# Destination lanes in source order: where a graph kernel scatters, gathers and counts

## The reference

```python
gate = silu(edge_attr @ F1W + F1b) @ F2W + F2b
gate = gate + (emb[atom_z[src]] * (emb[atom_z[dst]] @ adapt)).sum(-1, keepdims=True)
msg  = gate * h[dst] * (cw * node_mult[dst])[:, None]
agg  = segment_sum(msg, src); tot = segment_sum(node_mult[dst], src)
# then four attention layers over the same edges, an MLP layer with segment_sum over dst,
# and two more: out = segment_sum(x[row] * norm[:, None], col), norm from deg = count of edges per row
```

## Time and profile before

| | us |
|---|---|
| median of 3 runs | 19813.48 |
| lowest and highest | 19801.2, 19824.42 |
| span of the profiled execution, first to last instruction | 17009.2 |
| time of the profiled execution around its span | not listed in the profile |
| median less span | 2804.3 |

### The profile page before, as it was taken

The page is one execution under the profiler, slowest core; times in us unless marked ns, Lnnn a source line. Parts: engine busy times, 40 slices in busy tenths (PEclk is TensorE's granted clock), DMA queues, the critical chain, the costliest instruction groups (busy, mean ns, idle before and its releaser), DMA issues. The chain is left out here.

```text
span 17009.2 us, 405783 instructions
## 1 busy us (share of the span) xinstructions
PE 9949.2 (58%) x119882; PEld 7747.5 (46%) x119882; DVE 11124.4 (65%) x27289; ACT 5234.6 (31%) x15775; POOL 9202.6 (54%) x10645
## 2 busy tenths in 40 slices
PE   2000047777777647974896599569926666433454
PEld 1000024444444237864785488458824444333324
DVE  6830046777776767985897599759954555466757
ACT  0000012222222014651564266236613333221120
POOL 7777777777777104431442244124427777585270
PEclk9755555555555569987997899699958777756656
DMA  3833357677678437645663666276612222134445
GB/s 117 327 93 102 102 87 80 85 85 85 85 86 79 80 102 209 176 126 150 186 176 91 196 176 176 56 227 176 175 48 61 65 65 65 45 129 143 148 152 161
DMA packets 2548685, 2116.02 MB, mean 124 GB/s; under 512 B 418374, under 2 KB 2314590, under 8 KB 2541593
## 3 DMA queue, kind: packets, MB, share of 16 engines
q1 hardware_dynamic: 2225086, 1439.58, 31.2%
q0 software_dynamic: 309216, 539.46, 19.4%
q10 hardware_dynamic: 14216, 135.01, 2.3%
HBM read 1290.57 MB, written 726.03 MB: 119 GB/s over the span
## 5 line engine op out<-in xcount | busy, mean ns | idle before, releaser
L627 POOL DMA_INDIRECT attend_rows<-key_rows,attend_fetch_now x1824 | 1747.7, 958 | 2056.5 <-PE attend_seg L1670 1729.3
L1714 ACT ACTIVATE attend_hot<-attend_lane_hot,attend_share 128x128 f32<-128x128 fp8e4 x7296 | 2228.5, 388 | 1209.9 <-DVE attend_share L1737 976.5
L627 POOL DMA_INDIRECT edges_rows<-raw,edges_perm_now x1824 | 2007.5, 1101 | 629.1 <-issue 602.4
L627 POOL DMA_INDIRECT keys_rows<-table,keys_staged x1564 | 1658.6, 1060 | 471.0 <-issue 471.0
L1670 PE MATMUL attend_seg<-attend_rows,attend_hot 128*128 128x49 f32 x14592 | 1816.8, 278 | 122.9 <-ACT parts_layer L1718 85.7
L1670 PEld LDWEIGHTS attend_seg<-attend_rows,attend_hot 128*128 128x128 f32 x14592 | 1734.3, 195 | 207.1 <-issue 201.9
L627 POOL DMA_INDIRECT mlp_xin<-table,mlp_staged x1564 | 1511.3, 966 | 472.7 <-issue 469.3
L1044 PE MATMUL edges_ps_t<-ident,edges_attr 128*40 128x128 f32 x1824 | 425.4, 413 | 1861.6 <-ACT edges_attr L1099 1833.9
L633 POOL DMA_INDIRECT messages<-spread_out,spread_place_now x912 | 1027.9, 1127 | 385.9 <-issue 276.5
L1657 PE MATMUL attend_qx<-attend_table,attend_oht 128*128 128x90 bf16 x21888 | 1087.8, 207 | 124.8 <-DMA attend_oht<-src_hots 113.0
L1481 POOL COPY expand_table<-k 128x156 bf16 x912 | 289.3, 317 | 1602.4 <-issue 947.3
(11 more groups left out here) (517 smaller groups left out, 23761.4 us busy)
## 6 DMA issues: line engine op xcount, KB each, us to landing
key_rows<-expand_out SPq DMA_DIRECT2D x304, 624.0 KB
attend_ea<-edge_attrs SPq DMA_DIRECT2D x912, 160.0 KB
tally_rows<-messages SPq DMA_DIRECT2D x152, 864.0 KB, 4.8
attend_table<-q SPq DMA_DIRECT2D x1832, 67.5 KB
expand_oht<-dst_hots SPq DMA_DIRECT2D x304, 384.0 KB, 4.8
attend_oht<-src_hots SPq DMA_DIRECT2D x912, 128.0 KB
attend_lane_hot<-src_hots_by_edge SPq DMA_DIRECT2D x912, 128.0 KB
raw<-keys_rows ACTq DMA_DIRECT2D x46, 2176.0 KB
```

Source lines behind the costliest of these rows:

```text
L627: return nc.gpsimd.indirect_dma_start(out=out, out_offset=None, in_=table, in_offset=bass.IndirectOffsetOnAxis(ap=index, axis=0))
L1714: ins = nc.scalar.activation(hot[p][:, u, c, :], lane_hot8[r][:, u, c, :], ACT.Copy, scale=share[p][:, u, c:c + 1])
```

## The change

The edge pass no longer scatters destination lanes or counts. It keeps the lanes in source order in a tile `k.dl_a`, stored once at its end as a table of granules (`k.dloc_a`). The one-hot stage gathers that table by a new index, `k.origin`, the inverse of `k.place`: four gathers for a chunk of four supertiles, then a store to `k.dloc_b`, then the load as before; the store and load are issued by ScalarE. The index is made in the key stage, behind the sort, like the place map but with the roles of the two orders exchanged. The counts are made there too, behind the index, in 92 half chunks of 17 columns from lanes and blocks in order of the input. The clearing of `k.dloc_b` goes.

```diff
 def edge_keys
-        nowhere = sb("nowhere", [P, NS], BF16)
+        HC = C // 2
+        lane_hot = [both[:, b, 0:HC * P // 2].bitcast(BF16).rearrange("p (c l) -> p c l", l=P) for b in range(2)]
+        block_hot = [both[:, b, HC * P // 2:HC * (P + NT) // 2 + 1].bitcast(BF16)[:, 0:HC * NT].rearrange("p (c t) -> p c t", t=NT) for b in range(2)]
...
-            for q in range(GR):
-                sp.dma_start(k.dloc_b.rearrange("(p q n) a -> p q (n a)", p=P, q=GR)[:, q], nowhere[:]).then_inc(s_out, 16)
...
+            with pe.Fori(0, CHUNKS) as n:
+                for b in range(2):
+                    pe.wait_ge(s_lanes[b], n + 1)
+                    for c in range(HC):
+                        ins = t.matmul(hist[b][:, 0:NT], lane_hot[b][:, c, :], block_hot[b][:, c, :], start=(c == 0), stop=(c == HC - 1))
+                    ins.then_inc(s_cnt, 1)
...
+            dve.sem_inc(s_inv, 1)
...
+            for q in range(4):
+                dve.wait_ge(s_mm, 13 + q)
+                ch.step(v.tensor_scalar(level[0:UT, :], small[0:UT, 256:256 + KB], uoff[0:UT, q:q + 1], None, ALU.subtract))
+                ch.done(v.tensor_copy(jump[0:UT, :], small[0:UT, 320:320 + KB]))
+                for half in (slice(0, P // 2), slice(P // 2, P)):
+                    ch.done(v.tensor_tensor(under, rows_of(level[0:UT, :], P // 2), bc(k.iota[0:UT, half], KB), ALU.is_le))
+                    ch.done(v.tensor_tensor(under, under, rows_of(jump[0:UT, :], P // 2), ALU.mult))
+                    ch.done(v.tensor_reduce(at[0:UT, q, half], under, AX, ALU.add))
...
+            ch.done(v.tensor_tensor(k.origin[:], k.origin[:], part, ALU.add))
+            ch.done(v.memset(k.count[0][:], 0.0))
+            with dve.Fori(0, CHUNKS) as t:
+                for b in range(2):
+                    here = bass.ds((t * 2 + b) * HC, HC)
+                    v.tensor_tensor(lane_hot[b], bc(loc[1][:, here], P), rows_of(k.iota[:], HC), ALU.is_equal)
+                    v.tensor_tensor(block_hot[b], bc(blk[1][:, here], NT), rows_of(k.iota[:, 0:NT], HC), ALU.is_equal).then_inc(s_lanes[b], 1)
+                for b in range(2):
+                    dve.wait_ge(s_cnt, t * 2 + b + 1)
+                    ch.done(v.tensor_tensor(k.count[0][:], k.count[0][:], hist[b][:, 0:NT], ALU.add))
 def edge_pass
-                if live(n, 2):
-                    o = (s - 2) % TURN
-                    pool.wait_ge(s_dl, n - 1)
-                    pool.wait_ge(s_place, n - 1)
-                    for u in range(CHR):
-                        scatter(nc, k.dloc_b, place_now[:, o, u:u + 1], dl[o][:, u, :], NS * P - 1).then_inc(s_scat[o], 16)
...
+            sp.wait_ge(s_dl, CHN)
+            sp.dma_start(k.dloc_a.rearrange("(p r) c -> p (r c)", p=P), k.dl_a[:]).then_inc(s_kept_dl, 16)
+            sp.wait_ge(s_kept_dl, 16)
...
-                    pe.wait_ge(s_hot, n + 1)
-                    after(pe, s_added, n)
-                    for c in range(COL):
-                        ins = mm(ps_n[:, 0:NT], hot_d[:, c, :], hot_j[:, c, :], start=(c == 0), stop=(c == COL - 1))
-                    ins.then_inc(s_cnt, 1)
...
-                    after(act, s_scat[b], t * (16 * CHR))
-                    a(dl[b][:].rearrange("p u c -> p (u c)"), rows[b][:, :, DL], ACT.Copy).then_inc(s_dl, 1)
+                    a(k.dl_a[:, bass.ds(n * COL, COL)], rows[b][:, :, DL], ACT.Copy).then_inc(s_dl, 1)
...
-                    v.tensor_copy(place_now[:, s], k.place[:, bass.ds(n * CHR, CHR)]).then_inc(s_place, 1)
...
-                        dve.wait_ge(s_cnt, n)
-                        ch.done(v.tensor_tensor(k.count[0][:], k.count[0][:], ps_n[:, 0:NT], ALU.add))
-                    ch.step(v.tensor_tensor(hot_d[:], bc(r[:, :, DL], P), rows_of(k.iota[:], COL), ALU.is_equal))
-                    ch.done(v.tensor_tensor(hot_j[:], bc(r[:, :, DB], NT), rows_of(k.iota[:, 0:NT], COL), ALU.is_equal))
 def dst_hots
+            for n in range(2 * HALF):
+                after(pool, s_taken, n - 1)
+                for u in range(n * HCH, (n + 1) * HCH):
+                    gather(nc, lanes[:, u, :], k.dloc_a, k.origin[:, u:u + 1]).then_inc(s_got[n % 2], 16)
...
+            def put(n, b, t):
+                at = bass.ds(n * HCH, HCH)
+                act.wait_ge(s_got[b], (t + 1) * (16 * HCH))
+                act.sem_inc(s_taken, 1)
+                act.dma_start(k.dloc_b.rearrange("(u p) c -> p u c", p=P)[:, at, :], lanes[:, at, :]).then_inc(s_put[b], 16)
+            def load(n, b, t):
+                act.wait_ge(s_put[b], (t + 1) * 16)
+                act.wait_ge(s_bro, n * HCH - b * HCH + 1)
+                act.dma_start(row[b][:], k.dloc_b.rearrange("(a u p) c -> a u (p c)", a=1, p=P)[:, bass.ds(n * HCH, HCH), :]).then_inc(s_row[b], 16)
+            put(0, 0, 0)
+            with act.Fori(0, HALF - 1) as t:
+                put(t * 2 + 1, 1, t)
+                load(t * 2, 0, t)
+                put(t * 2 + 2, 0, t + 1)
+                load(t * 2 + 1, 1, t)
...
-                    sp.dma_start(lanes[:, at, :], k.dloc_b.rearrange("(u p) c -> p u c", p=P)[:, at, :]).then_inc(s_lanes, 16)
```

More of the change, by code:

```diff
@@ L423, in _ @@
             ins.then_inc(s_perm, 1)
+            pe.wait_ge(s_inv, 1)
+            t.transpose(small[0:NT, 128:128 + NT], base[0][0:NT, 0:NT], k.ident[0:NT, 0:NT]).then_inc(s_mm, 1)
+            for q in range(4):
+                pe.wait_ge(s_inv, 2 + q)
+                t.matmul(small[0:UT, 256:256 + KB], ended[0:NT, q * UT:(q + 1) * UT], base[1][0:NT, :], start=True, stop=True)
+                t.matmul(small[0:UT, 320:320 + KB], ended[0:NT, q * UT:(q + 1) * UT], steps[0:NT, :], start=True, stop=True).then_inc(s_mm, 1)
+            pe.wait_ge(s_inv, 6)
+            for q in range(4):
+                ins = t.transpose(wide[:, q * UT:(q + 1) * UT], at[0:UT, q, :], k.ident[0:UT, 0:UT])
+            ins.then_inc(s_mm, 1)
+            with pe.Fori(0, CHUNKS) as n:
[4 more added lines that the diff above has]
+                    ins.then_inc(s_cnt, 1)
         @block.vector
@@ L582, in _ @@
             ch.done(v.tensor_scalar(listed, listed, float(E), None, ALU.min))
+            dve.sem_inc(s_inv, 1)
+            dve.wait_ge(s_mm, 12)
+            ch.done(v.tensor_tensor(shift[0:NT, 0:NT], small[0:NT, 128:128 + NT], base[1][0:NT, 0:NT], ALU.subtract))
+            ch.step(v.tensor_scalar(begun[0:NT, :], uiota[0:NT, :], first[1][0:NT, :], None, ALU.is_ge))
+            ch.step(v.tensor_copy(steps[0:NT, 0:1], shift[0:NT, 0:1]))
+            ch.step(v.tensor_tensor(steps[0:NT, 1:NT], shift[0:NT, 1:NT], shift[0:NT, 0:NT - 1], ALU.subtract))
@@ new lines, in _ @@
+            ch.done(v.tensor_tensor(tot[1][0:NT, :], final_b[0:NT, :], lane[0:NT, :], ALU.add))
+            ch.done(v.tensor_scalar(ended[0:NT, :], uiota[0:NT, :], tot[1][0:NT, :], None, ALU.is_gt))
+            ch.done(v.tensor_tensor(ended[0:NT, :], begun[0:NT, :], ended[0:NT, :], ALU.subtract))
+            dve.sem_inc(s_inv, 1)
+            for q in range(4):
+                dve.wait_ge(s_mm, 13 + q)
[5 more added lines that the diff above has]
+                    ch.done(v.tensor_reduce(at[0:UT, q, half], under, AX, ALU.add))
+                ch.done(v.tensor_tensor(at[0:UT, q, :], at[0:UT, q, :], gran[0:UT, q, :], ALU.add))
+                dve.sem_inc(s_inv, 1)
@@ L1214, in _ @@
                 step(CHN + s, s, LOOPS)
-            dve.wait_ge(s_cnt, CHN)
-            ch.done(v.tensor_tensor(k.count[0][:], k.count[0][:], ps_n[:, 0:NT], ALU.add))
             dve.wait_ge(s_ev, CHN)
```

70 lines of the change are left out of this document (33 added, 37 removed).

## The result

| | median us | lowest, highest | runs |
|---|---|---|---|
| before | 19807.34 | 19799.03, 19824.42 | 4 |
| after | 19640.99 | 19627.19, 19660.36 | 4 |

The account below looks back on a forecast made before the run. GpSimd was taken to bound the key stage and edge pass, VectorE's comparisons the one-hot stage. Edge pass -260, final store +3, one-hot stage +221 and key stage +200 make +164 us on 19813.5: 19978 us, range 19790 to 20150.

Parts of the forecast that it names:

- the gain of the edge pass: Edge pass: 210 us for late records plus 60 less 10 gives 260 us, bounds 120 and 443.
- a floor of 12.78 us a step: Edge pass: the loop of TensorE and ScalarE allows no less than 228 x 12.78 = 2914 us.
- Which I carry unchanged: Whole kernel: the median's 2804.3 us above the profiled span was taken to stay the same.
- Key stage: Key stage: new VectorE instructions with two SBUF inputs hold GpSimd's gathers, about +200 us, bounds 0 and 260.
- Rival D: Key stage: the new comparisons don't hold the gathers, so it costs nothing; 19777 us in all, chance 0.07.
- the scatters': Edge pass: without scatters GpSimd stops being the bound; 210 us of late records credited in full.
- The count: Edge pass: removing it lets VectorE catch up faster after stalls, 60 us, bounds 0 and 119.
- Rival C: Edge pass: stalls are absorbed and it runs at its 12.78 us loop, winning 443 us; 19795 us in all, chance 0.12.
- Rival B: Edge pass: DMA queues take over, broadcast-load stalls leave a gain of only 120 us; 20118 us in all, chance 0.15.
- One-hot stage: One-hot stage: 456 gathers at 1.25 us on GpSimd set its length, 588 us for 367, +221 us.
- rival E: One-hot stage: three DMAs in sequence per chunk make 1.5 us a gather, +330 us; 20087 us in all, chance 0.11.
- Nothing else in the span is edited: Whole kernel: only the key stage, edge pass and one-hot stage are touched by the change.

Follow-up runs that it names:

- e1: The kernel before, unedited, profiled a second time, on a slow chip: 19367.05 us.
- e12: The kernel before, unedited, once more on a third slow chip: 19915.18 us.
- e18: Changed kernel with the count back in the edge pass (lanes only), and a step's eight gathers parted by a wait, quick chip: 0.9875 of before.
- e10: The whole change, unedited, against the kernel before, on a slow chip: 1.0088.
- e13: Changed kernel with the eight count matmuls of a step kept in the edge pass on constant one-hots, unused, slow chip: 0.9889 of before.
- e4: The changed kernel, unedited, against the kernel before, on a quick chip: 16803.74 us, 0.9902.
- e7: Changed kernel without the edge pass's record gathers, on constant records (output not the reference's), quick chip: 16754.92 us in one run.
- e16: Changed kernel with a step's eight record gathers parted by a wait for VectorE's dot product, quick chip: 0.9908 of before.
- filler: Changed kernel with the count's matmuls or its comparisons back in the edge pass, unused; quick chip: 0.9915 (matmuls), 0.9928 (comparisons) of before.
- e9: Kernel before with only the counts moved to the key stage, scatters kept, slow chip: 1.0274 of before.
- e15: Changed kernel without the edge pass's record gathers, on constant records (output not the reference's), slow chip: 18579.08 us in one run.
- e11: Changed kernel with the key stage's count one-hots made column by column, by comparisons with a per-partition scalar, slow chip: 1.0268 of before.
- e8: Changed kernel with the count back in the edge pass, so only the lanes are moved, slow chip: 0.9922 of before.
- e14: Changed kernel with the two count comparisons of a step kept on VectorE in the edge pass, unused, slow chip: 0.9903 of before.

## Why the prediction was wrong

In short: on the quick chips, from which the prediction's rows come, the step that failed is the gain of the edge pass, forecast as 260 us at a floor of 12.78 us a step and measured as 553. On the chip of the first result, where the kernel of before wasn't profiled, the cause is inferred from other slow chips; the end of this section says how.

**The base.** "Which I carry unchanged" was the first error. The 2804.3 us between median and span were no fixed surround: the traced execution's time is its span plus 2 us (19660.36 and 19658.6). They were the difference between two kinds of chip. Between the earlier trace rows and e1 it is 974 us in the MLP stage, 697 in the edge pass (1134 in e12), 366 in the attention stages, 203 in the last stage with scatters and 127 in the key stage. What follows compares with the quick chip, whose stages are those of the earlier trace rows.

**Key stage, right.** Forecast +200 (43 for the map, 156 for the count); measured +195, with 45 for the map (e18) and 150 for the count. Rival D is out. The slow chips show +154 (e1 to e10) and +159 (e12 to e13), from a stage that already took 122 to 127 us longer.

**Edge pass, the step that failed.** Forecast -260, measured -553. The floor of 228 x 12.78 us was no floor. The step in the earlier trace rows was a common one at TensorE's lower clock. Steps of 10.2 us were in the same trace:

```profile
2711.70 1.86 PE L1044 MATMUL edges_ps_t<-ident,edges_attr 128*40 128x128 f32 x8 [1.50 <-ACT edges_attr L1099]
...
2714.55 2.21 PE L1061 MATMUL edges_ps<-edges_w,edges_act 49*128 49x48 f32 x16
...
2721.95 1.86 PE L1044 MATMUL edges_ps_t<-ident,edges_attr 128*40 128x128 f32 x8 [1.50 <-ACT edges_attr L1099]
```

The gate matmuls took 2.21 us there and 3.65 a step earlier. The windows of the two steps have the granted clock behind the busy times, 0.50 (1.2 GHz throughout) and 0.69 (2.4 GHz for part of the step):

```profile
2701.00:2712.00 11.00, 9.50 (x61) 6.04 (x60) 8.92 (x24) 2.36 (x6) 8.68 (x7) 0.50 0.56 105
2713.00:2722.00 9.00, 7.50 (x64) 4.59 (x63) 7.52 (x22) 3.67 (x8) 6.87 (x8) 0.69 0.66 54
```

Before, 32 of 227 steps took under 11.8 us; in the changed kernel 108 of 227 (e4), at a mean clock of 0.57 for 0.53. There, as without gathers (e7), short and long steps take turns, 10.2 us at a clock of 0.67 and 13.5 us at 0.50:

```profile
3504.00 1.87 PE L1093 MATMUL edges_ps_t<-ident,edges_attr 128*40 128x128 f32 x8 [1.95 <-ACT edges_attr L1142]
3514.22 1.87 PE L1093 MATMUL edges_ps_t<-ident,edges_attr 128*40 128x128 f32 x8 [1.95 <-ACT edges_attr L1142]
3527.76 1.87 PE L1093 MATMUL edges_ps_t<-ident,edges_attr 128*40 128x128 f32 x8 [1.95 <-ACT edges_attr L1142]
```

Why the clock changes from step to step isn't shown. So the loop of TensorE and ScalarE takes 11.9 us on the mean when nothing else is late (e7), and not 12.78, and the floor is 2746 us, the pass without gathers; the change came within 57 us of it. By an estimate from these steps, 280 to 380 of the 553 us are the 76 steps that became short ones (each 3.7 to 5.0 us shorter, by the mean long step after or before), and the rest is long steps that fell from 15.3 to 13.9 us. A floor has to be taken from the shortest steps at both clocks, or from their mix, not from one step.

The term inside it that was mis-sized is the scatters': 210 us were credited, and lanes only won 452 (3356 to 2904). (The 2904 are those of e18, which has e16's wait; in the changed kernel that wait made 5 us.) The wait at L1044 in the earlier trace rows was turned into a gain as if every other step stayed at 12.78 us; the steps that are short at the higher clock aren't in it. (Its sum also took 226 waits of 1.50 us where the row has 214.) The count was credited 60 and brought 101 (2904 to 2803), of which a filler shows 35 to be VectorE's comparisons; the other 66, which the fillers leave out with the count's waits and add, aren't assigned. Rival C had the mechanism, a pass at the loop of TensorE and ScalarE, and with 443 us the size of the wrong floor. Rival B is out: the load stalls fell from the 59 (263.3 us) of the earlier trace rows to 6 (28.9 us between 2600 and 5200 us of e4), although the DMA's rate rose from 83 to 99 GB/s.

**One-hot stage, right on the quick chip.** Forecast 588, measured 608. On slow chips it is 679 to 692, rival E's size (361 + 330 = 691). A gather still takes 0.95 us, with 0.30 to the next where nothing holds it, and the rest is waiting for ScalarE's queue, as in this row of the first result:

```profile
L686 POOL DMA_INDIRECT hots_lanes<-dst_lanes_by_src,origin x456 | 431.3, 946 | 239.3 <-issue 152.4 <-ACTq L1279 83.5 <-remote 3.4
L1336 DVE TENSOR_SCALAR hots_oht<-hots_ps_b,hots_lane 128x512 fp8e4<-128x512 f32 x456 | 312.2, 744 | 375.8 <-issue 193.3 <-PE hots_ps_b L1322 172.3 <-DMA dst_hots<-hots_oht 9.9
```

**"Nothing else in the span is edited" left out 78 us.** Each of the four expansion stages became some 20 us shorter, on every chip and in every kernel with the lanes moved, and in none without. They are bound by the DMA queues (shares of 0.95 and 1.00 below), and the same bytes go faster, first before, then e4:

```profile
6239.00:6517.00 278.00, 157.56 (x5472) 151.40 (x5472) 135.73 (x455) 75.98 (x228) 72.34 (x228) 0.97 0.95 280
```

```profile
6123.00:6381.00 258.00, 158.56 (x5472) 152.37 (x5472) 135.96 (x456) 75.95 (x228) 72.81 (x228) 0.96 1.00 302
```

Why wasn't tried; the change adds a table in DRAM ahead of those tensors and takes SyncE's clearing away.

**The sum.** Quick chip: 195 - 553 + 246 - 78 = -190, the spans differ by 189. Slow chips with before at 19367 (e1 and e10, on two chips): 154 - 230 + 323 - 78 = +169, against +83 between their spans (the rest is other stages and differences of the two executions) and +150 between the medians. That this is near the forecast of +164 is luck: its terms were 200, -260 and 221, and the one-hot and the expansion stages, 102 and 78 us off, nearly cancel, and so do the key stage and the edge pass, -46 and +30. On the chip of the first result before wasn't profiled. Its time, 19807, lies near the 19915 of e12, whose edge pass was in the loop of ten descriptors; 3844 less 4490, with the other stages, would be -240. On the chip of e12 the changed kernel with either filler was faster too, 0.989 and 0.990, with an edge pass that fell by 634 and 612 us. That the first result is faster because before was caught in that loop there is inferred from this, not shown.

## What to carry to other kernels

Compare a profile's span with the measured time before using its durations: if they differ by more than a few us (2 us here), the profile is of other conditions, and sums from it can't be carried over. Where an engine goes at two clocks, look for the shortest period of a loop in the trace as well as the typical one before calling it a floor. And where a producer writes descriptors in long rows and others wait for the row to end, a descriptor less per step shortens the step by at least its own time: from counts only (e9) to the whole change (e10) a row went from 12.5 to 9.9 us and a step from 19.6 to 16.7.

## What the runs showed of the hardware

- The same program took 16959 to 16982 us on three chips, and 19367, 19367 and 19915 on three others, each within 0.8%. The difference is in stages with gathers: MLP 2036 or 3010 to 3081 us, edge pass 3356 or 4052 to 4490; the stages without them are equal (one-hots 362 and 361, tallies 602 and 602).
- On the slow chips instructions come in steps of about 0.70 us while GpSimd issues gathers. In the key stage 42 to 47% of SyncE's register instructions took over 0.3 us, on the quick chips none. The ninetieth percentile of its register moves in the edge pass was 0.21 to 0.69 us, but 0.03 on a quick chip, and 0.03 too on the slow chip without gathers (e15). In the one-hot stage it was 0.03 in e1, which has no gathers there, and 0.70 in the first result, which has. VectorE's 1.40 us in e11 is twice 0.70, and falls to 0.20 behind the last gather. What of the gathers causes it stays open.
- A gather that GpSimd issues within a long VectorE instruction on SBUF ends 0.8 us after that instruction, on both kinds of chip. In the kernel before this held for instructions with two SBUF inputs (L566, 3.96 us a gather on the mean), for a copy from SBUF to SBUF (L157, 1.23 us long, gathers of 1.65) and for the comparison by scalar (L1167, 0.75 us long, gathers up to 1.45). It didn't for a reduction (L568, 3.49 us long, gathers of 0.95), nor for copies from PSUM (0.94). The Trainium skill (SBUF — State Buffer, Who interferes with whom) infers that writing descriptors is spared by an instruction with two SBUF inputs; the timeline of the changed kernel shows again that such a gather isn't, whichever part of its work waits.
- Lanes alone and counts alone (e8, e9) change the slow chip's edge pass by -410 and +445 us against e1, both together (e10) by -230. The pass is 180 us longer without the count (3822 and 3642), and neither filler gives that back. The traces show where it arises: with the count in the pass the dot product starts ahead of the end of GpSimd's row in 79 of 222 rows of e8 (0.03 us behind it on the mean, at rows of 11.1 us), and without it in none of e9, e10, e13 and e14 (1.4 to 2.0 us behind). Why the count has this effect is open.
